# Scores as plain fp32 products in two row tiles, the attention result divided with its channels on partitions

## The reference

```python
x = x + _L0_attn_ref(_layernorm(x), Wq, Wk, Wv, Wo)     # 16 heads of 8 channels
x = x + _L0_ffn_ref(_layernorm(x), ...)                 # 16 experts of 64, 4 per token, and a shared one

# attention: blocks of 64 queries see the keys of their own and the previous block, inside a band
mask = (j > i) & (j <= i + W)
scores = where(mask, einsum('bhnqd,bhnkd->bhnqk', qb, k2) * scale, -1e30)
out = einsum('bhnqk,bhnkd->bhnqd', softmax(scores, axis=-1), v2)

# router: sigmoid scores, the best 2 of 4 groups, then the best 4 experts, weights scaled to a sum of 2.5
y = einsum('ne,enh->nh', combine, einsum('enm,emh->enh', silu(x @ w_gate) * (x @ w_up), w_down))
return y + (silu(x @ sw_gate) * (x @ sw_up)) @ sw_down
```

## Time and profile before

| | us |
|---|---|
| median of 3 runs | 815.47 (813.79 to 815.57) |
| the profiled execution: its time | 814.36 |
| the profiled execution: span of the trace | 812.6 |
| busy: TensorE, its weight loads | 740.3, 611.7 |
| busy: GpSimd, ScalarE, VectorE | 618.8, 607.7, 525.1 |
| TensorE's mean granted clock, share of full | 0.977 |

### The profile page before, as it was taken

How to read it: one execution, slowest core, us unless ns; L and a number is a source line. 1 busy time by engine, 2 the same in 40 slices (tenths; PEclk the granted TensorE clock), 3 DMA queues, 4 the chain that set the end, 5 groups by cost and what they waited for, 6 DMA issues and landing times.

```text
span 812.6 us, 19809 instructions
## 1 busy us (share of the span) xinstructions
PE 740.3 (91%) x5984; PEld 611.7 (75%) x5984; DVE 525.1 (65%) x1735; ACT 607.7 (75%) x1816; POOL 618.8 (76%) x842
## 2 busy tenths in 40 slices
PE   2568889999999999999999999999999999998876
PEld 1446668787887878787887878787887878786755
DVE  3456686767767676767667676767767575764332
ACT  4787788788787888878788788878787888863332
POOL 3525467879888888978888888988888887956876
PEclk9698899999999999999999999999999999999999
DMA  5000022040413213040312213040313203041321
GB/s 155 26 1 15 14 74 73 15 136 10 120 40 97 63 53 105 2 133 22 105 52 92 65 42 115 2 129 26 105 52 90 67 31 114 3 122 37 117 92 41
DMA packets 50738, 53.86 MB, mean 66 GB/s; under 512 B 5632, under 2 KB 31744, under 8 KB 50560
## 3 DMA queue, kind: packets, MB, share of 16 engines
q1 hardware_dynamic: 50688, 53.25, 21.5%
HBM read 44.31 MB, written 4.72 MB: 60 GB/s over the span
## 4 chain that ended last, share of the span: by engine, by line
PE 45%; POOL 26%; issue 16%; ACT 8%; DMA 2%; DVE 2%; POOLq 1%; SPq 0%; ACTq 0%; DVEq 0%
POOL gate L470 9%; PE PS L1053 8%; PE PS L979 7%; PE PS L869 7%; PE PS L911 6%; PE PS L870 5%; PE PS L871 5%; ACT probs L602 4%; POOL hh L473 4%; POOL q_lo L452 4%; POOL k_lo L462 2%; PE PS L972 2%; PE PS L1050 2%; POOL X L432 1%; PE PS L1014 1%
## 5 line engine op out<-in xcount | busy, mean ns | idle before, releaser
L602 ACT ACTIVATE probs<-PS,neg_max 128x96 f32<-128x96 f32 (+1 forms) x1024 | 245.8, 353 | 60.1 <-DVE neg_max L798 59.4
L470 POOL TENSOR_TENSOR gate<-gate,spread 128x512 f32<-128x512 f32 x128 | 164.2, 1283 | 64.4 <-DMA spread<-weights_by_expert 47.2
L750 DVE STREAM_TRANSPOSE probsT<-probs 128x384 f32<-128x384 f32 (+1 forms) x256 | 124.0, 522 | 101.8 <-ACT probs L602 101.8
L473 POOL TENSOR_TENSOR hh<-gate,tu 128x512 f32<-128x512 f32 x128 | 164.5, 1285 | 17.2 <-POOL gate L470 11.9
L786 DVE SCALAR_TENSOR_TENSOR tu<-th,PS 128x512 f32<-128x512 f32 x128 | 87.9, 687 | 89.3 <-PE PS L871 56.4
L1053 PE MATMUL PS<-wd,hh 128*128 128x128 f32 x1024 | 136.1, 276 | 9.6 <-POOL hh L473 9.6
L1053 PEld LDWEIGHTS PS<-wd,hh 128*128 128x128 f32 x1024 | 126.6, 192 | 15.1 <-POOL hh L473 9.4
L798 DVE TENSOR_REDUCE neg_max<-PS 128x4 f32<-128x384 f32 (+1 forms) x256 | 125.4, 513 | 8.2 <-PE PS L979 5.4
L869 PE MATMUL PS<-x_hi,w_hi 128*128 128x512 f32 x288 | 125.0, 434 | 1.0 <-DVE hs L834 1.0
L560 ACT ACTIVATE th<-PS 128x512 f32<-128x512 f32 x128 | 79.7, 623 | 59.6 <-PE PS L871 59.2
L871 PE MATMUL PS<-x_lo,w_hi 128*128 128x512 f32 x288 | 114.5, 397 | 0.0
(11 more groups left out here) (108 smaller groups left out, 1362.1 us busy)
## 6 DMA issues: line engine op xcount, KB each, us to landing
spread<-weights_by_expert SPq DMA_DIRECT2D x256, 128.0 KB, 3.0
X<-x SPq DMA_DIRECT2D x32, 256.0 KB, 3.4
OUT<-H SPq DMA_DIRECT2D x16, 256.0 KB, 3.0
out<-OUT SPq DMA_DIRECT2D x16, 256.0 KB, 3.1
probsT<-w_gu SPq DMA_DIRECT2D x1, 1152.0 KB, 8.0
wd<-w_down SPq DMA_DIRECT2D x1, 512.0 KB, 9.0
weights_by_expert<-cT SPq DMA_DIRECT2D x16, 32.0 KB, 1.6
probsT<-w_att SPq DMA_DIRECT2D x1, 264.0 KB, 3.5
```

The source lines that it names most:

```text
L470: tt(gate2[:, :], gate[:, k % 2, :], spread[:, k % SP_BUFS, :], ALU.mult).then_inc(s_g2, 1)
L473: tt(hh[:, k % 2, :], gate2[:, :], tu[:, k % 2, :], ALU.mult).then_inc(s_h, 1)
L602: ins = nc.scalar.activation(probs[:, u % 2, tt, a, j0:KW], PS[:, tt, a * KW + j0:a * KW + KW], ACT.Exp, bias=neg_max[:, tt, a:a + 1])
L750: ins = v_.transpose(probsT[:, b, :, t0 + tt, c0:3, :].rearrange("p g c q -> p g (c q)"), probs[:, u % 2, tt, :, c0 * Q:KW])
```

## The change

Scores: the queries are copied out of PSUM once, in plain fp32, four times with a quarter of a channel mask and the scale (`q_by_head`), the keys twice, by halves of the key groups (`k_by_row`). Channels 0 to 63 and 64 to 127 are now two row tiles of TensorE: each has the products of its own half of the heads, 2 groups x 96 keys, into its own PSUM bank. So a bank holds both tiles of queries for half of the heads, and the scores of a unit start when all exponentials of the unit before are done. High and low copies of queries and keys go. The keys are projected for both sequences at once.

Result: PV multiplies by values and by a column block of ones in separate products, in four column tiles of 32. The result has channels on partitions, and the sums have the same partitions: VectorE takes reciprocals of 128 x 256 and multiplies out of PSUM into `oT` (stages ON, 15 and 19). Four stages and six transposes of a sequence go.

Moves: LN1 from 0 to 3, XT from 1 to 4, QP from 2 to 5, KP to 6, VP to 6, PV from 11 to 12; on GpSimd the last routing part goes ahead of `hh`, the others ahead of LN2. At the start GpSimd makes the low part of the feed-forward weights (128 x 2304), which VectorE did.

```diff
@@ -39,19 +39,13 @@
 
 
 
-LN1 = 0
-XT = 1
-QP, VP, VB = 2, 5, 6
-QC = (4, 8)
-QC_LOW = (4, 9)
-KP = (6, 8)
-KC = (7, 10)
-KC_LOW = (7, 11)
+LN1 = 3
+XT = 4
+QP, KP, VP, VB = 5, 6, 6, 7
 SC = 8
 TR = 9
-PV = 11
-OE = 13
-OT, ON, OW = 14, 15, 16
+PV = 12
+ON, OW = 15, 16
 LN2 = 17
 XT2 = 19
...
+                    g, _ = at(sl, s, QP)
+                    if g:
+                        if g.fixed and g.n == 0:
+                            act.wait_ge(s_pool, 8)
+                        side, bank = filled(act, sl, s, LATE)
+                        for v in range(4):
+                            ins = copy(q_by_head[:, g.par, :, v, :], blocks(bank), scale=queryrow[:, v:v + 1])
+                        ins.then_inc(s_taken[side], 1)
+                    g, _ = at(sl, s, KP)
+                    if g:
+                        side, bank = filled(act, sl, s, LATE)
+                        for e in range(2):
+                            ins = copy(k_by_row[:, g.par, e, :], bank, scale=keyrow[:, e:e + 1])
+                        ins.then_inc(s_taken[side], 1)
...
+                    g, b = at(sl, s, ON, 4, GB)
+                    if g:
+                        dve.wait_ge(s_o_ps, g.n * GB + b + 1)
+                        link(sl, v_.reciprocal(o_rs[:, :], PS[:, 2, T:2 * T]))
+                        v_.tensor_tensor(oT[:, :], PS[:, 2, 0:T], o_rs[:, :], ALU.mult).then_inc(s_o, 1)
...
-                                pt = probsT[:, b, a, :, :, :].rearrange("p t c q -> p (t c) q")
-                                r0, c0 = 64 * (a % 2), T * (a // 2) + Q * kb
-                                ins = mm(PS[r0:r0 + 64, 2, c0:c0 + Q * nq],
-                                         v_bd[:, g.par, b * NQ + kb, a, :, :].rearrange("p k f -> p (k f)"),
-                                         pt[:, 3 * kb + 2:3 * kb + 2 + 2 * nq - 1:2, :],
-                                         start=(kb == 0 and a < 2), stop=(kb == NQ - 1), skip_group_check=True)
+                            for ones in (False, True):
+                                for a in range(HG):
+                                    pt = probsT[:, b, a, :, :, :].rearrange("p t c q -> p (t c) q")
+                                    c0 = T * ones + Q * kb
+                                    ins = mm(PS[32 * a:32 * a + 32, 2, c0:c0 + Q * nq],
+                                             headcol if ones else v_bd[:, g.par, b * NQ + kb, a, :],
+                                             pt[:, 3 * kb + 2:3 * kb + 2 + 2 * nq - 1:2, :],
+                                             start=(kb == 0 and not ones), stop=(kb == NQ - 1), skip_group_check=True)
...
+                            taken(pe, slot_before(sl), QP % STEPS, LATE)
+                            taken(pe, slot_before(sl), KP % STEPS, LATE)
+                        if not (g.fixed and g.n == 0 and u == 0):
+                            pe.wait_ge(s_p, 2 * (g.n * NU + u))
+                        quarters = [slice(64 * rows, 64 * rows + 64) for rows in range(2)]
+
+                        def hide(n0, n1, which, first, step, start):
+                            for rows, r in enumerate(quarters):
+                                dst = PS[:, rows, 0:4 * KW].rearrange("p (n k) -> p n k", n=4)[:, n0:n1, :]
+                                hidden = slice(first, KW // Q, step)
+                                mm(blocks3(dst)[:, :, hidden, :], ident4[r, :],
+                                   blocks2(band[r, which, :])[:, hidden, :].unsqueeze(1).broadcast_to(
+                                       [64, n1 - n0, len(range(3)[hidden]), Q]),
+                                   start=start, stop=False, skip_group_check=True)
+
+                        if u % 4 == 0:
+                            hide(0, 2, 1, 1, 1, True)
+                            hide(2, 4, 0, 2, 1, False)
+                        else:
+                            hide(0, 4, 0, 0, 2, True)
                         for tt in range(2):
                             t = 2 * (u % 4) + tt
                             nk = min(KW, (t + 1) * Q)
                             q1 = (u // 4) * T + (t + 1) * Q
+                            for rows, r in enumerate(quarters):
+                                dst = PS[:, rows, 2 * KW * tt:2 * KW * tt + 2 * KW].rearrange("p (e k) -> p e k", e=2)
                                 ins = mm(dst[:, :, KW - nk:KW],
+                                         q_by_head[r, g.par, q1 // Q - 1, :, :].rearrange("p v q -> p (v q)"),
+                                         k_by_row[r, g.par, :, q1 - nk:q1], start=False, stop=(tt == 1),
+                                         skip_group_check=True)
+                                if tt == 1:
+                                    ins.then_inc(s_s, 1)
```

In the same way `o_rs` becomes 128 x 256, and `keys`, `q_lo`, `k_lo`, OE, OT and the transposes of ON are taken out on every engine. At the start:

```diff
+                    if sl.fixed and sl.n == 0 and s == PREPARE:
+                        pool.wait_ge(s_cst, 3)
+                        tt(w_lo[:, WG:W_COLS], ffn_stage, w_hi[:, WG:W_COLS].bitcast(F32),
+                           ALU.subtract).then_inc(s_cst, 1)
```

More of the change, by code:

```diff
@@ L144 @@
 W_COLS = WU + NF * P
-LOADS, FFN_LOADS = 4, 4
-PREPARE = 4
+LOADS, FFN_LOADS = 5, 4
+PREPARE = 7
 ORDER_PER_SLOT = 5
@@ L541, in slot @@
                         act.wait_ge(s_cst, 2)
-                        copy(w_hi[:, WG:W_COLS], stage[:, WG:W_COLS]).then_inc(s_cst, 1)
-                    def keys(b):
-                        g, _ = at(sl, s, KP[b])
-                        if g:
-                            side, bank = filled(act, sl, s, KEY_PLACE[b])
-                            if not (g.fixed and g.n == 0 and b == 0):
-                                act.wait_ge(s_k_hi, g.n * GB + b)
-                            copy(kr_hi[:, :], bank[:, 0:T]).then_inc(s_high[side], 1)
-                    keys(0)
+                        copy(w_hi[:, WG:W_COLS], ffn_stage).then_inc(s_cst, 1)
                     g, _ = at(sl, s, LG)
@@ L578, in slot @@
                         nc.scalar.activation(th[:, :], PS[:, 4, :], ACT.Tanh, scale=0.5).then_inc(s_th, 1)
-                    keys(1)
-                    g, _ = at(sl, s, QP)
-                    if g:
-                        if not (g.fixed and g.n == 0):
-                            act.wait_ge(s_q_hi, g.n * GB)
-                        side, bank = filled(act, sl, s, LATE)
-                        copy(qr_hi[:, :], bank, scale=Q_SCALE).then_inc(s_high[side], 1)
                     g, _ = at(sl, s, XT)
@@ L761, in slot @@
                                      ).then_inc(s_taken[side], 1)
-                    def keys(b):
-                        g, _ = at(sl, s, KP[b])
-                        if g:
-                            side, bank = high_out(sl, s, KEY_PLACE[b])
-                            if not (g.fixed and g.n == 0 and b == 0):
-                                dve.wait_ge(s_k_lo, HG * (g.n * GB + b))
-                            split_low(kr_lo[:, :], bank[:, 0:T], kr_hi[:, :]).then_inc(s_taken[side], 1)
                     g, _ = at(sl, s, YE)
@@ L970, in slot @@
-                            first, step = (Q, Q) if t == 0 else (j0 + Q, Q) if j0 else (0, 2 * Q)
-                            hidden = slice(first // Q, KW // Q, step // Q)
-                            mm(blocks3(dst)[:, :, hidden, :], ident4[:, :],
-                               blocks2(band[:, int(t == 0), :])[:, hidden, :].unsqueeze(1).broadcast_to(
-                                   [P, HG, len(range(3)[hidden]), Q]),
-                               start=True, stop=False, skip_group_check=True)
```

273 lines of the change are left out of this document (76 added, 197 removed).

## The result

The changed kernel takes 853.06 us (median of 5 runs, 847.2 to 854.15), the kernel before 814.43 (5 runs): 1.0458 times as long, interval 1.0437 to 1.048. The forecast was 805, its outer range 782 to 850. It is 4.6% slower with less work on every engine but VectorE: TensorE is busy 728.9 us instead of 740.3, ScalarE 516.0 instead of 607.7, GpSimd 479.4 instead of 618.8. Head of the page of the changed kernel: busy time by engine, and the clock granted to TensorE in 40 slices.

What follows compares the result with a forecast made beforehand. TensorE's work plus its waits was taken to bound the kernel, with VectorE late next. 812.6 - 4 (steady state) - 5 (filling) - 1 (emptying) = 802.6, plus 1.8 outside the span: 804, said as 805; forecast range 795 to 815, outer 782 to 850.

Steps and rivals of the forecast that it cites:

- 42.2 us a slot: TensorE's work per period after the change: 46.0 - 1.3 - 1.0 - 0.2 - 0.1 - 1.2.
- Values: Products with values on TensorE: 32 records in four column tiles, four at once, 0.81 us as before; -0.2 a period.
- Scores: TensorE's scores in two row tiles: 0.12 masks, 0.67 products, 0.34 change of tiling, 1.13 a full step; -1.0 a period.
- rival B: TensorE's tiles do not overlap: values +4.4 a period, 850 us; if row tiles fail, +5.6 on scores, 856; chance 0.17.
- 2.8 at `tu`: Step 3: TensorE waits 2.8 us a period for VectorE's `tu`, ahead of the shared expert's product.
- the reciprocals: VectorE's reciprocals, grown from 32 to 256 a partition: 1.65 us taken, bounds 0.42 and 2.76.
- 0.65 at the router: Step 7: TensorE waits 0.65 us a period for VectorE's low part of x2, ahead of the router's product.
- wait for `comb`: TensorE's wait in step 3 for GpSimd's `comb`, claimed to go: -1.2 us a period.
- Rivals A: Reciprocals cost VectorE only 0.42 us and do not hold TensorE: period 43.8, 783 us; chance 0.15.
- C: Reciprocals on VectorE cost 2.76 us, waits grow by 1.1 each: period 47.9, 832 us; chance 0.08.
- Period: 42.2 + 2.8 + 0.65 = 45.65: Steady-state period as TensorE's work plus its waits in steps 3 and 7, against 46.0: -4 us over twelve.
- Filling: The stretch before the steady state: -5 us in all, first scores 2 to 3 us earlier.

Runs made afterwards that it cites:

- e3: The changed kernel with the closing branch of TensorE's loop announced at the head of each pass: 837.14 us, 1.0291 of the kernel before.
- e5: The changed kernel's new scores with the result path of the kernel before, closing branch of TensorE's loop announced: 786.28 us, 0.9661 of the kernel before.
- e11: The changed kernel with the closing branch announced and the reciprocals split in two halves, the second half and the product behind `tu`: 794.27 us, 0.9764.
- e10: The kernel before, instruction for instruction, with the head of TensorE's loop laid at slot 208 of a block of instructions: 826.46 us, 1.0167.
- e2: The changed kernel with VectorE's reciprocals, product and statistics of X moved behind `tu` of the same step: 861.51 us, 1.0596 of the kernel before.

## Why the prediction was wrong

**TensorE's work: right.** 42.2 us a slot were forecast. A slot of e3 with the clock at 1.00 throughout shows what the program does undisturbed, though blocks are fetched in it too; below it stand a later one with 3.4 us and one with 6.8 us of half clock:

```profile
354.60:399.90 45.30, 41.90 (x509) 32.97 (x508) 33.20 (x107) 31.80 (x96) 29.58 (x36) 1.00 0.23 69
447.10:494.10 47.00, 43.60 (x510) 34.35 (x509) 33.29 (x107) 31.80 (x96) 29.55 (x36) 0.96 0.23 71
494.10:542.60 48.50, 45.11 (x510) 35.30 (x509) 33.54 (x106) 31.89 (x96) 29.54 (x36) 0.93 0.22 65
```

41.9 of work and 45.3 in all, where the sum gave 42.2 and 45.65. Values: 0.79 for 0.81 forecast. Scores: 1.07 a full step for 1.13, with the change of tiling in both; of the 0.34 taken for it 0.28 came. So both halves of rival B are out. That its 850 and 856 lie beside the measured 853 is chance. The rule of the Trainium skill (TensorEngine Tiling (Array Packing), Key Properties) that a change of mode drains TensorE would show here as the 0.10 ahead of the scores and the 0.11 behind them.

**The new waits: right.** 2.69 to 2.81 for 2.8 at `tu`, 0.70 for 0.65 at the router, the reciprocals 1.73 for 1.65; no wait for `comb` in the steady state. Rivals A and C are out by the reciprocals' time.

**The step that failed is the last one, "Period: 42.2 + 2.8 + 0.65 = 45.65".** It adds work at full clock to waits. The text named the danger (a 2.8 us wait could cost the clock for a while) as something that would show the forecast wrong, and gave it no price and no share in the range. Its price is 47.0 - 45.3 = 1.7 us for each half-clock stretch of 3.4 us, and up to two lie in a slot: the changed kernel without the stop at the branch took 837.14, with both places filled by idle work 815.21, and with 1.4 us waits 794.27 (779.4 with the division left out).

**A second step was not there at all: TensorE's program as something to be fetched.** "Values: 16 records become 32 ... no change" priced the records where they run. They also lengthen the loop from 1617 to 2128 records, and this loop is fetched again in each pass; that its length is the reason, and not its place, was not tested apart. Each return to the head costs 2.45 us of standing still, in which the 0.7 us of wait at the router disappear, and 6.8 us at half clock, some 3.4 more: 52.1 - 46.9 = 5.2 us in every second slot. The earlier trace rows show nothing of it. The pages have a row for it (queue, packets, MB, share), first of before, then of the changed kernel, and I had not read it:

```profile
q8 instruction: 24, 0.39, 0.2%
```

```profile
q8 instruction: 72, 1.18, 0.6%
```

The ten slots of 491.4 us by these terms: 10 x 45.3 undisturbed, 10 x 1.6 (46.9 - 45.3) for the clock behind `tu`, 1.6 for the second stretch of the one slot of 48.5, 4 x 5.2 for the fetch and its clock: 453 + 16 + 1.6 + 20.8 = 491.4.

**The ends.** From the first scores of the fourth group to those of the sixteenth it is 551.8 us before and 586.5 now: +34.7, where -4 was forecast. Filling came to -1.2 (135.9 us for 137.1 up to that fourth group) where -5 was taken: the first scores start 6.8 us earlier (18.5 for 25.3) and not 2 to 3, but the next group's follow 41.5 us later and not 34.8. Emptying gave -0.7 for -1.

The clock and the fetch made the sign wrong. Of the change's halves the scores gain (e5: 814 to 786) and the result path loses: 51 us as it is placed (e3 against e5), 8 at its best placing (e11 against e5).

## What to carry to other kernels

Where a change lengthens an engine's loop, count the instructions of a pass and look for instruction blocks on the DMA queues inside the loop: if they appear, announce the closing branch or move the loop's head, one line each, 16 to 27 us here, and look again whether the blocks or only the stop at the branch went. A wait on TensorE is to be priced with the half clock that can follow it (1.7 us more for most of the 2.7 us waits here), so a late operation on another engine is worth splitting until the wait is short, as the two halves of the reciprocals were. And a part that saves work on its own engine is best tried apart from a part that adds a wait elsewhere.

## What the runs showed of the hardware that I had not expected

- The same 1672 records of TensorE's loop were fetched in every pass (4.1 to 4.6 us at the branch) or in none (0.22 to 0.24), by the place of the loop's head alone: 813.1 against 786.76 us. In e10 the fetching stopped by itself after two slow branches and a third fetched pass.
- Idle products in TensorE's waits made the program 21 us faster (836.67 to 815.21), by the clock.
- A wait of TensorE of 1.9 to 2.0 us (e2) was enough for a half-clock stretch behind it in nearly every slot, while 2.70 us in one slot of e3 brought none.
- Four column tiles took 32 records of fp32 products in 0.79 us, and two row tiles eight records of 192 columns in 0.74 (459.19 - 458.45), where one after the other they would take 1.34 (eight at the 0.167 of the prediction).
